# A GRU and FFN kernel: six input products of the exact steps are moved into the unused row half of the recurrent products' low adds

## What is computed

```python
gi = x @ W_ih + b_ih
gh = h @ W_hh + b_hh
i_r, i_z, i_n = jnp.split(gi, 3, axis=-1)
h_r, h_z, h_n = jnp.split(gh, 3, axis=-1)
r = jax.nn.sigmoid(i_r + h_r)
z = jax.nn.sigmoid(i_z + h_z)
n = jnp.tanh(i_n + r * h_n)
h_new = (1.0 - z) * n + z * h
```

## Time and profile before

| | |
|---|---|
| median of 3 runs | 5935.98 us (5935.13 to 5938.93) |
| the profiled execution | 5935.94 us, span 5934.1 us |
| PE busy | 5107.1 us, 86% of the span |
| DVE, ACT, POOL busy | 49%, 31%, 29% |
| mean granted clock of PE | 0.952 of full |

### The profile page before, as it was taken

How to read it: one execution, slowest core, us unless ns; L and a number is a source line. 1 busy time by engine, 2 the same in 40 slices (tenths; PEclk the granted TensorE clock), 3 DMA queues, 4 the chain that set the end, 5 groups by cost and what they waited for, 6 DMA issues and landing times. The chain is left out here.

```text
span 5934.1 us, 232765 instructions
## 1 busy us (share of the span) xinstructions
PE 5107.1 (86%) x102020; PEld 3343.8 (56%) x102020; DVE 2915.2 (49%) x5649; ACT 1824.6 (31%) x4050; POOL 1739.0 (29%) x801
## 2 busy tenths in 40 slices
PE   0299999999999999999999999999960599996665
PEld 0177766666666666666666667777650244442222
DVE  5244434447763444544464446426538311128887
ACT  4022222222222223522262226425502311114443
POOL 0133323333332331233213330441241000006776
PEclk9999999999999999999999999999985799998777
DMA  4411111111111111311131113544533100000111
GB/s 110 95 48 46 49 37 49 46 45 48 47 50 37 47 48 51 93 49 46 44 104 46 49 44 97 142 118 119 143 81 115 33 24 22 24 18 21 28 28 34
DMA packets 262286, 352.18 MB, mean 59 GB/s; under 512 B 47134, under 2 KB 214343, under 8 KB 261257
## 3 DMA queue, kind: packets, MB, share of 16 engines
q1 hardware_dynamic: 259689, 333.29, 20.4%
q0 software_dynamic: 1760, 5.77, 0.3%
HBM read 303.19 MB, written 28.33 MB: 56 GB/s over the span
## 5 line engine op out<-in xcount | busy, mean ns | idle before, releaser
L628 PE MATMUL psum<-whole_w,whole_hot 128*32 128x384 f16 x49152 | 3005.6, 327 | 27.0 <-issue 27.0
L635 PE MATMUL psum<-low_w,low_hot 128*32 128x384 f16 x24576 | 2100.2, 327 | 0.0
L628 PEld LDWEIGHTS psum<-whole_w,whole_hot 128*32 128x32 f16 x49152 | 1379.6, 97 | 653.8 <-issue 30.4
L577 ACT ACTIVATE whole_w<-run_high 32x384 f16<-32x384 f32 x1488 | 777.3, 522 | 2204.0 <-DVE run_high L784 2191.1
L522 POOL TENSOR_TENSOR whole_hot<-whole_a,whole_mask 48x2048 f16<-48x2048 f16 x192 | 692.8, 3609 | 2197.2 <-PE psum L628 1666.3
L784 DVE TENSOR_SCALAR run_high<-psum 128x384 int32<-128x384 int32 x372 | 207.6, 558 | 1593.7 <-PE psum L628 1500.3
L635 PEld LDWEIGHTS psum<-low_w,low_hot 128*32 128x32 f16 x24576 | 689.6, 97 | 312.1 <-issue 0.7
L674 PE MATMUL psum<-low_w,low_hot 64*64 64x384 f16 x20480 | 845.2, 323 | 21.3 <-DMA low_w<-w_rows 13.7
L791 DVE TENSOR_SCALAR whole_w<-psum 32x384 f16<-32x384 f32 x1488 | 821.9, 552 | 27.8
L674 PEld LDWEIGHTS psum<-low_w,low_hot 64*64 64x64 f16 x20480 | 635.0, 107 | 231.1 <-DMA low_w<-w_rows 36.1
L592 ACT ACTIVATE low_hot<-low_a,sum_scale 128x128 f16 x1536 | 469.8, 388 | 304.6 <-PE psum L674 267.1
(11 more groups left out here) (269 smaller groups left out, 3619.9 us busy)
## 6 DMA issues: line engine op xcount, KB each, us to landing
low_w<-w_rows SPq DMA_DIRECT2D x640, 144.0 KB
whole_w<-w_rows SPq DMA_DIRECT2D x768, 72.0 KB
low_w<-w_rows SPq DMA_DIRECT2D x384, 120.0 KB
low_w<-w_rows SPq DMA_DIRECT2D x640, 48.0 KB
low_w<-w_rows SPq DMA_DIRECT2D x384, 72.0 KB
w_rows<-w_split SPq DMA_DIRECT2D x128, 144.0 KB
work<-in_x SPq DMA_DIRECT2D x64, 128.0 KB, 2.6
out_y<-work SPq DMA_DIRECT2D x64, 128.0 KB, 2.3
```

Of the source, the lines that this page charges most:

```text
L577: last = nc.scalar.activation(whole_w[0:Q, buf, u * 2 + half, bq, :], run_high[own, u, :], ACT.Copy, scale=1.0 / HIGH_ONE)
L628: last = nc.tensor.matmul(run[m][u][j * Q:(j + 1) * Q, :], whole_hot[:, buf, sign, kk, j % 2 * Q:(j % 2 + 1) * Q], whole_w[:, buf, u * 2 + ...
L635: nc.tensor.matmul(run[m][u][j * Q:(j + 1) * Q, :], low_hot[:, buf, kk, j % 2 * Q:(j % 2 + 1) * Q], low_w[:, buf, cols(j // 2, u)], start= ...
```

## The change

The chains become one list, `MAINS`: x0, h0, x1, h1, ..., h7, ten in all. The first six are fine. Each of them carries a **rider**, one of the six input products x5, x6, x7, x2, x3, x4 (`RIDERS`) that had a sum chain of its own. In a fine chain `add_low` now puts the main product's low pieces of both groups of eight terms into rows 0 to 63 and the rider's pieces into rows 64 to 127; the same four matmuls a kk and u are now 64 rows x 64 columns: two for the main tile, two for the rider's. `add_whole` is as it was. `low_w` is twice as wide, since both groups stand in the same rows. The riders' gate values stay in `gates_x` until their step. Rider operands are turned inside the fine chains, after block 1 (and the next main one after block 2 of the first two chains). A product of the sum kind now takes 8 places in `pick` and not 16, and its copies are shared by ACT and DVE (`place_second`).

```diff
+MAINS = ((0, 0), (0, 1), (1, 0), (1, 1), (2, 1), (3, 1), (4, 1), (5, 1), (6, 1), (7, 1))
+RIDERS = (5, 6, 7, 2, 3, 4)
+FINE = len(RIDERS)
+CUT_FROM = 5
...
-                low_w = ssb("low_w", [P, BUFS, G3], F16)
+                low_w = ssb("low_w", [P, BUFS, SUBS * G3], F16)
...
-                run = [[psum[:, 2 * m + u, 0:UC] for u in range(2)] for m in range(2)]
+                RIDER, MAIN = 0, 1
+                run = [[psum[:, 2 * slot + u, 0:UC] for u in range(2)] for slot in range(2)]
...
+                part_of = (slice(B, 2 * B), slice(0, B))
...
+                                if i < FINE:
+                                    x_src = w_rows[bass.ds(c, 1)].rearrange("a r n -> r (a n)")
+                                    for first, rows_of, loads in ((0, src, LOW_LOADS), (B, x_src, SUM_LOADS)):
+                                        for row, kind, kinds in loads:
+                                            both = rows_of.rearrange("(s r) n -> r s n", s=SUBS)
+                                            sp.dma_start(low_w[first + row * SK:first + (row + kinds) * SK, buf, :].rearrange("p (s n) -> p s n", s=SUBS),
                                                          both[kind * SK:(kind + kinds) * SK]).then_inc(w_in[buf], 16)
...
-                                if fine:
-                                    nc.gpsimd.tensor_tensor(
-                                        low_hot[:, buf],
-                                        low_a[:, bass.ds(c + m * NBK, 1), 0, :].to_broadcast([P, BK, B]),
-                                        low_mask[:].unsqueeze(2).to_broadcast([P, BK, B]),
-                                        ALU.mult).then_inc(hot_ok, 1)
-                                else:
...
+                                nc.gpsimd.tensor_tensor(
+                                    low_hot[:, buf].rearrange("p (s k) b -> p s k b", s=SUBS),
+                                    low_a[:, bass.ds(c, 1), :, :].rearrange("p a s b -> p (a s) b").unsqueeze(2).to_broadcast([P, SUBS, SK, B]),
+                                    sum_mask[:].unsqueeze(1).unsqueeze(3).to_broadcast([P, SUBS, SK, B]),
+                                    ALU.mult).then_inc(hot_ok, 1)
...
+                        def place(i, slot):
+
+                            for n in range(PB):
+                                a.wait_ge(selected[slot], (places(i) if slot == MAIN else PB * i) + (n + 1))
+                                for rows, sub in ((part_of[slot], 0), (part_of[slot], 1)) if i < FINE else ((part_of[0], 0), (part_of[1], 0)):
+                                    last = nc.scalar.activation(low_a[rows, n::PB, sub, :], picked(n, sub), ACT.Copy)
+                                last.then_inc(placed[slot], 1)
...
-                        def x_one_hots(t):
-                            chain = chain_no(t, 0)
-
-                            def make(c, buf):
...
-                                for k in range(SK):
-                                    last = nc.scalar.activation(low_hot[:, buf, k::SK, :],
-                                                                low_a[:, bass.ds(c, 1), :, :].rearrange("p a s b -> p (a s) b"),
-                                                                ACT.Copy, scale=sum_scale[:, k:k + 1])
-                                last.then_inc(hot_ok, 1)
...
                             def add_low(u, buf, kk):
-                                for j in range(4):
-                                    nc.tensor.matmul(run[m][u][j * Q:(j + 1) * Q, :], low_hot[:, buf, kk, j % 2 * Q:(j % 2 + 1) * Q],
-                                                     low_w[:, buf, cols(j // 2, u)],
-                                                     start=False, stop=True, skip_group_check=True)
+                                for slot in (MAIN, RIDER):
+                                    rows = part_of[slot]
+                                    for half in range(2):
+                                        at = kk // SK * G3 + (u * 2 + half) * UC
+                                        nc.tensor.matmul(run[slot][u][half * B:(half + 1) * B, :], low_hot[rows, buf, kk, :], low_w[rows, buf, at:at + UC],
+                                                         start=False, stop=True, skip_group_check=True)
...
+                                for job in between.get(c, ()):
+                                    job()
...
-                        turn_x(0, 0)
-                        pick(0, 0, True)
-                        turn_x(1, 1)
-                        fine_chain(0, 0)
-
-                        def step(t, fine, x_fine):
-                            turn_h(t)
-                            if x_fine is not None:
-                                pick(t + 1, 0, x_fine)
-                            pick(t, 1, fine)
-                            if x_fine is not None:
-                                pe.wait_ge(gates_ok[0], t * 2 + 2)
-                                turn_x(t + 2, 0)
-                            (fine_chain if fine else sum_chain)(t, 1)
-                            if x_fine is not None:
-                                pe.wait_ge(a_split_ok[0], t + 3)
-                                (fine_chain if x_fine else sum_chain)(t + 1, 0)
-
-                        for t in range(EXACT):
-                            step(t, t < H_FINE, t + 1 < X_FINE if t + 1 < EXACT else None)
+                                last.then_inc(selected[slot], 1)
+                            pe.wait_ge(placed[slot], at + (2 * PB if whole else PB))
+                            if slot == MAIN and not whole:
+                                pe.wait_ge(placed_second, PB * (i - FINE + 1))
+
+                        turn_main(0)
+                        turn_rider(0)
+                        for i, (t, m) in enumerate(MAINS):
+                            if i < FINE:
+                                pick(i, RIDER)
+                            if m == 1 and t > 0:
+                                turn_main(i)
+                            pick(i, MAIN)
+                            if i < FINE:
+                                jobs = {}
+                                if i + 1 < FINE:
+                                    jobs[1] = (lambda: turn_rider(i + 1),)
+                                    if i < 2:
+                                        jobs[2] = (lambda: turn_main(i + 1),)
+                                fine_chain(i, jobs)
+                            else:
+                                sum_chain(i)
...
+                        def place_second(i):
+
+                            for n in range(PB):
+                                v.wait_ge(selected[MAIN], places(i) + (n + 1))
+                                for rows in part_of:
+                                    last = nc.vector.tensor_copy(low_a[rows, n::PB, 1, :], picked(n, 1))
+                                last.then_inc(placed_second, 1)
...
+                                    next_base(i, c, c % BUFS, u)
+                                    if c >= CUT_FROM:
+                                        for _ in range(pace):
+                                            next(work, None)
...
-                        finish(cut_pieces(0, 0, 0))
-                        first_bases(0, 0)
-                        fine_bases(0, 0, cut_pieces(1, 0, 1), 1)
-
-                        def step(t, fine, x_fine):
-                            finish(cut_pieces(t, 1, 1))
-                            if fine:
-                                first_bases(t, 1)
-                            gate_values(t, 0)
-                            next_x = cut_pieces(t + 2, 0, 0) if x_fine is not None else iter(())
-                            if fine:
-                                fine_bases(t, 1, next_x, 1)
-                            finish(next_x)
-                            gate_values(t, 1)
-                            work = elementwise(t)
-                            if x_fine:
-                                first_bases(t + 1, 0)
-                                fine_bases(t + 1, 0, work, WEAVE)
-                            finish(work)
-
-                        steps(v, step)
...
+                        finish(cut_pieces(0, MAIN))
+                        finish(cut_pieces(0, RIDER))
+                        v.wait_ge(bias_in, 64)
+                        for i, (t, m) in enumerate(MAINS):
+                            if m == 1 and t > 0:
+                                finish(cut_pieces(i, MAIN))
+                            if i < FINE:
+                                first_bases()
+                                if i < 2:
+                                    chain_bases(i, in_turn(cut_pieces(i + 1, RIDER), cut_pieces(i + 1, MAIN)), 1)
+                                elif i == 2:
+                                    chain_bases(i, in_turn(cut_pieces(i + 1, RIDER), elementwise(0)), WEAVE)
+                                elif i + 1 < FINE:
```

(18 more changed lines are left out.)

373 lines of the change are left out of this document (170 added, 203 removed).

## The result

The changed kernel takes 7292.73 us (median of 4 runs, 7289.86 to 7296.40) against 5935.56 us before: ratio 1.2288, 95% interval 1.2266 to 1.2309. The forecast was 7303. The profiled execution took 7289.86 us, its span is 7287.8.

What follows compares the result with a forecast made beforehand. PE bounds the kernel, alone within the fine chains. Changes of form +1475, x chains -134, start +9, early gaps +13 and turns +4 sum to +1367 on 5935.94 us: 7303 us, range 7050 to 7600.

Steps and rivals of the forecast that it cites:

- Changes of form: Fine chains: low sets of 64*64 between whole sets of 128*32 lengthen each of 6144 steps by 0.24 us, +1475 us.
- all else in the chains: Fine chains: seven operand turns inside them cost about 0.6 us each, +4 us; loads and other engines' work cost nothing.
- What it is: Fine chains: at a change of form weight loads don't run under the set before and the engine drains; part of +1475.
- Free changes: Rival for the fine chains: changes between these two forms cost nothing, 5828 us, faster by 1.8%; chance 10%.
- all the other parts: Whole kernel apart from the price of changes of form: 108 us less, 5936 - 108 = 5828 us.
- The clock falls: Rival for the fine chains: PE granted 1.2 GHz for 2.4, a step 1.22 us, 10,300 us; chance 3%.
- The six x chains: Between the chains of h1 to h7: six sum chains go, gate arithmetic lies bare, 573.7 against 707.7, -134 us.
- Gaps after sum chains: Pieces before h5, h6 and h7: gates, turn, cuts, pick and first operands make 92.7 us each.
- Early gaps: Three gaps between the first chains: a rider pick and a full pick each, 81.3 for 68.1, +13 us.
- The sum: Whole kernel: 1475 - 134 + 9 + 13 + 4 = +1367 us on 5935.94, 7303 us.
- the rest: Ahead of x0's chain +9 us for the rider's cuts and pick; chains of h4 to h7 and all behind, 0.

Runs made afterwards that it cites:

- e1: Changed kernel with low adds back as four matmuls of 128 rows x 32 columns, riders' adds left out: 5833.9 us, ratio 0.9831 to the kernel before.
- e3: Changed kernel with the steps of a block half grouped in pairs, half as many changes of form: 6563.2 us, ratio 1.1059 to the kernel before.
- e6: Changed kernel with the 16 steps of a block half taken together, 768 changes of form for 12,288: 5924.5 us, ratio 0.9982 to the kernel before.
- e2: Changed kernel with each low set as eight matmuls of 64 rows x 32 columns, four a tile: 7287.4 us, ratio 1.2279 to the kernel before.
- e4: Kernel before with each low set of a fine chain as two matmuls of 128 rows x 64 columns, for four of 128 x 32: 7381.5 us, ratio 1.2437.
- e5: Changed kernel without the riders' two matmuls of each low set, two of 64 x 64 left: 10,327.5 us, ratio 1.7399 to the kernel before.
- e11: Changed kernel without riders' adds, the main product's low adds as four matmuls of 64 rows x 32 columns: 10,204.4 us, ratio 1.7196 to the kernel before.

## Why the prediction was right, point by point

- *Changes of form.* The term that decides was read from three pairs of forms that the trace of before has, none of them the pair of the change. It was forecast at 0.24 us a step and 1475 us, and measured at 0.238 and 1464 with all else in the chains. The runs e1, e3 and e6 show it as a price a change, e2 and e4 that it is owed for rows and for columns alike. That a pair which was not in the trace would pay what three others do was an assumption of the forecast, which held.
- *What it is.* That loads don't run ahead over a change, read off, is borne out by the 0.318 us of idle PEld a low set. That the array drains was argued: a change cost 0.12 us whatever the shape beside 128\*32, and 0.13 at half the clock, but no run separates the empty array from the late load.
- *Free changes* (10%): what e1 measures, 5834 us, is this rival's 5828. It was wrong for the changed kernel, but its amount, the worth of all the other parts, was right.
- *The clock falls* (3%): it did not in the changed kernel, 1.00 in the chains. The reason I gave against it, that the clock was low only in windows with idle times of microseconds, agrees with e5 too, where it fell in the 5.4 us ahead of the chain. What I had not thought of is that a chain can fail to get it back: e5 and e11 have PE busy for all of 1200 us at 0.50. The rival had the cause in the times without a stream; the changed kernel has these as e5 has, and came back to full.
- *The six x chains.* -134 forecast, -129 measured: with the shared copies the 8 places of a sum product took 10.1 us and the last copies 1.0 (h4's pick from 5131.11, its clear at 5142.21), where I had 9.4 and nothing. Gaps after sum chains are 94.2 for 92.7.
- *Early gaps.* +13 forecast, +21 measured: 27.2 us where I had 25.3. Each of the two low picks there took 7.64 us for 7.15, and PE waited 0.86, 0.38 and 0.47 us for copies of ACT, which now makes two half copies a place of a low pick.
- *Not forecast:* the chains of h4 to h7 took 86.0, 86.4, 84.5 and 83.3 us before, and now 83.3 each, 7 us less in all, which is most of the -8. In part that is seen: PE waited for loads of `low_w` in the first three, for 1.7, 0.3 and 0.8 us, and in h5's chain the granted clock was 0.98; in the changed kernel it waits for no load there. Where the rest went, and why the loads come in time, is not shown.
- *The sum.* It is 10 us off the median, and 13 in the trace. Measured less forecast, its terms are off by -15 in the chains, +5 and +8 in the gaps, -4 and -8 in the rest. They cancel in part, and so far the closeness is luck; the mechanism does not hang on it.

The window of the kernel before over h5's chain:

```profile
3915.10:4001.50 86.40, 85.91 (x2048) 68.65 (x2048) 13.23 (x12) 7.34 (x24) 59.77 (x31) 0.98 0.51 136
```

## What to carry to other kernels

Count how often neighbouring matmuls change the rows x columns they use of the array: each change cost 0.119 us here, three quarters of a set of 384 columns, and was paid 12,288 times to be rid of some 13,000 matmuls. Work that fills an empty corner of the array cost nothing here where its matmuls stood among others of their shape (e6), and 0.12 us at each change where they did not; three other pairs of shapes in the trace of before gave that price ahead of the run. And before a hidden piece is taken away, read how long the thing behind it is: here 85 us of x chain came off a path on which 75 us of gate arithmetic stood ready to take its place.

## What the runs showed that I had not expected

Taking work out of PE kept its clock low. With rows 64 to 127 empty in one set of three, beside two changes of form a step, the granted clock, which falls in the idle time ahead of each chain in all these kernels, stayed at 1.2 GHz through the fine chains although a matmul was under way all the time, and the kernel took 10,204 to 10,327 us; with matmuls on those rows too, the rider's (64\*64, 64\*32) or the main product's own (128\*64), it came back to 2.4 GHz, and the kernel took 7272 to 7293 us. The Trainium skill, page "TensorE: Matmul & The Clock Gate", section "Part 1: The HAM clock gate", has it that the gate follows how busy PE has been. In the profile's sense of busy the two kernels at 1.2 GHz don't agree with that, since PE is busy for all of their windows; what the gate takes for busy was not measured. Also new to me: a set of eight matmuls takes no longer than one of four (e2), and a change costs nearly the same at both clocks.
